# Adaptive layer norm, a state-space mixer and a top-2 mixture of experts: sixteen slots, a new beginning, statistics a step ahead, W2's sums and scaling moved

## The reference, cut to what matters

```python
mod = (silu(c) @ wmod).reshape(16, 6, 1, 128)        # sa, ca, ga, sb, cb, gb per sequence
h = layernorm(x) * (1 + ca) + sa
xi = silu(h @ Win + bin)                             # 256 channels
# h_t = 0.9 h_{t-1} + xi_t Bp;  y_t = h_t Cp + Dp xi_t   (a scan over 512 tokens)
x = x + ga * (y @ Wout + bout)
h = layernorm(x) * (1 + cb) + sb
p = softmax(h @ Wr + br); probs, idx = top_k(p, 2)   # 8 experts
for every expert e: r = layernorm(relu(h @ W1[e] + b1[e])) * g1[e] + be1[e]      # 512 wide
                    y_e = layernorm(relu(r @ W2[e] + b2[e])) * g2[e] + be2[e]    # 128 wide
x = x + gb * (sum over the two chosen experts of gate * y_e)
```

## Time and profile before

| what | value |
|---|---|
| median of 3 runs | 551.77 us (550.8 to 551.81) |
| the profiled execution, its own time | 549.6 us |
| its span, first to last instruction | 547.8 us |
| busy: TensorE, VectorE, ScalarE, GpSimd | 489.3, 472.3, 400.9, 384.5 us |
| mean granted TensorE clock | 0.969 of full |
| beginning, to the scan of batch 0 | 0 to 28.4 us |
| mixer, to the scan of batch 15 | 28.4 to 171.6 us |
| turn to the experts | 171.6 to 190.9 us |
| experts' tiles | 190.9 to 520 us |
| the end | 520 to 547.8 us |

### The profile page before, as it was taken

How to read it: one execution, slowest core, us unless ns; L and a number is a source line. 1 busy time by engine, 2 the same in 40 slices (tenths; PEclk the granted TensorE clock), 3 DMA queues, 4 the chain that set the end, 5 groups by cost and what they waited for, 6 DMA issues and landing times. The chain is left out here.

```text
span 547.8 us, 15172 instructions
## 1 busy us (share of the span) xinstructions
PE 489.3 (89%) x3075; PEld 389.0 (71%) x3075; DVE 472.3 (86%) x2217; ACT 400.9 (73%) x1107; POOL 384.5 (70%) x524
## 2 busy tenths in 40 slices
PE   2698897989896589899999999999999999999863
PEld 2264554555554469699999999999989899889740
DVE  5968899898988578598888899999999899999896
ACT  1435877587876357688888888888888798888763
POOL 4361477777777777866665668888888788769683
PEclk9999999999999589999999999999999999999996
DMA  6962011451111165454555555666666766666665
GB/s 176 309 186 77 31 54 50 95 111 54 55 50 54 55 174 134 136 151 138 143 146 145 173 144 177 179 187 161 182 186 151 181 193 159 184 182 195 189 180 154
DMA packets 79342, 77.81 MB, mean 142 GB/s; under 512 B 11086, under 2 KB 72681, under 8 KB 79126
## 3 DMA queue, kind: packets, MB, share of 16 engines
q1 hardware_dynamic: 70838, 59.92, 42.0%
q0 software_dynamic: 8416, 16.93, 8.7%
HBM read 54.65 MB, written 22.59 MB: 141 GB/s over the span
## 5 line engine op out<-in xcount | busy, mean ns | idle before, releaser
L577 POOL DMA_INDIRECT expert_results<-y,target x135 | 136.3, 1010 | 42.3 <-issue 41.0
L546 POOL DMA_INDIRECT expert_rows<-rows_ring,slot x128 | 123.4, 964 | 54.8 <-issue 53.6
L1344 PE MATMUL bank<-W,h2T 128*128 x1080 | 142.7, 275 | 0.7 <-ACT h2T L727 0.7
L1344 PEld LDWEIGHTS bank<-W,h2T 128*128 128x128 f32 x1080 | 131.2, 192 | 0.9 <-issue 0.9
L719 ACT ACTIVATE h1T<-bank 128x512 f32<-128x512 f32 x135 | 80.7, 598 | 44.6 <-PE bank L1329 43.6
L1108 DVE BATCH_NORM_STATS2 stf<-h1T 128x6 f32<-128x512 f32 x135 | 90.9, 673 | 0.0
L1335 PE MATMUL bank<-ident,h1T 128*128 128x128 f32 x540 | 80.9, 272 | 0.0
L1335 PEld LDWEIGHTS bank<-ident,h1T 128*128 128x128 f32 x540 | 67.3, 141 | 18.2
L727 ACT ACTIVATE h2T<-bank 128x512 f32<-128x512 f32 x135 | 79.6, 589 | 0.0
L1326 PE MATMUL bank<-b_parts,onesr 128*128 x135 | 65.3, 484 | 3.2 <-DVE h3lo L1100 3.2
L1084 DVE SCALAR_TENSOR_TENSOR wmod<-bank,rse,shifts 128x128 f32<-128x128 f32 x135 | 46.5, 344 | 20.5 <-PE bank L1344 7.1
(11 more groups left out here) (212 smaller groups left out, 1037.7 us busy)
## 6 DMA issues: line engine op xcount, KB each, us to landing
shifts<-expert_shifts SPq DMA_DIRECT2D x135, 192.0 KB
hrow<-expert_rows SPq DMA_DIRECT2D x135, 65.0 KB
xi<-expert_results SPq DMA_DIRECT2D x12, 512.0 KB, 5.1
X<-in_L_attn_x SPq DMA_DIRECT2D x8, 512.0 KB, 7.1
out_x<-X SPq DMA_DIRECT2D x15, 256.0 KB
expert_results<-y,target POOLq DMA_INDIRECT x135
shifts<-in_L_ffn_W SPq DMA_DIRECT2D x4, 512.0 KB, 6.4
expert_rows<-rows_ring,slot POOLq DMA_INDIRECT x128, 2.3
```

The source lines that it names most:

```text
L546: nc.gpsimd.indirect_dma_start(out=rows_d, out_offset=bass.IndirectOffsetOnAxis(ap=slot[q][:, n // TOPK, n % TOPK:n % TOPK + 1], axis=0), ...
L577: nc.gpsimd.indirect_dma_start(out=results_d, out_offset=bass.IndirectOffsetOnAxis(ap=target[n % TURN][:], axis=0), in_=y[k][:], in_offset ...
L1344: ins = mm(acc, rT[q][:, ch * P:(ch + 1) * P], W2[:, bass.ds(e2 * CF + ch, 1), :], start=(ch == 0), stop=(ch == CF - 1))
```

## The change

- **Sixteen slots.** Up to tile 31 shifts and y have 16 slots (`ring(i)`), the second eight in tiles that the mixer no longer needs (xi, mixT, scan, spare_gb). Semaphores of these loads and stores serve pairs of slots (`pair`, `pair_uses`). target has 32 buffers.
- **First round.** Four batches instead of three: 24 tiles. GROUP_ENDS is (4, 7, 10, 13, 14, 15, 16) instead of (3, 5, 8, 11, 14, 15, 16). GpSimd stores all rows of the last batch at once, with y additions of tiles 0 to 11 between the last two batches' stores, and stores two results per addition for tiles 12 to 17.
- **Pieces of the sum.** The 44 early pieces lie evenly over tiles 52 to 132 (`piece_tile`), loads and stores of X in SyncE's list follow them.
- **New beginning.** b1_parts is zeroed by ScalarE instead of GpSimd, b2_rows after VectorE's constants; c and wmod have semaphores of their own; X's first 256 KB come before the small loads and the next 256 KB behind them; batch 0's statistics and root come before the modulation (`first_norm`, `first_mods`); the modulation's products go to bank 4.
- **Statistics a step ahead.** The first statistics of batch s+3 stand between the dependent operations of step s's chain (`first_stats`, `first_mv`). n2 of batch s-1 is normalised in step s, half before h1T and half behind it, instead of in step s+1.
- **W2.** Sums one expert per step in steps 2 to 9, in bank 4, copied in two halves in steps 6 and 10 (`copy_sums`). Scaling in steps 12 to 18, five pieces a step between other operations (`scale_w2`).
- **half_gates.** The tanh and the table load of the gates stand behind the first h3hi instead of ahead of the experts.

The diff, cut to its core:

```diff
...
-    ROUND1_BATCHES = 3
-    GROUP_ENDS = (ROUND1_BATCHES, 5, 8, 11, 14, 15, 16)
+    ROUND1_BATCHES = 4
+    GROUP_ENDS = (ROUND1_BATCHES, 7, 10, 13, 14, 15, 16)
...
-        target = [sb(f"target_{n}", [P, 1], I32) for n in range(8)]
+        TARGETS = 32
+        target = [sb(f"target_{n}", [P, 1], I32) for n in range(TARGETS)]
...
+        FIRST_COMBINED, LAST_COMBINED = 52, EXPERT_TILES - 3
...
+        def piece_tile(b, j):
+            return FIRST_COMBINED + (b * J + j) * (LAST_COMBINED - FIRST_COMBINED) // (EARLY * J - 1)
+        def pieces_at(i):
+            return [(b, j) for b in range(EARLY) for j in range(J) if piece_tile(b, j) == i]
...
+        WIDE_UNTIL = 32
...
+        y += [xi_flat[0][:, n * D:(n + 1) * D] for n in range(RESULTS)]
+        mix_flat = mixT_both[:].rearrange("p q l -> p (q l)")
+        shift_rows = [shifts[:, n, :] for n in range(SLOTS)]
+        shift_rows += [of[:, n * 3 * D:(n + 1) * 3 * D] for of in (xi_flat[1], mix_flat) for n in range(2)]
+        shift_rows += [scan[0][:, 0:3 * D], scan[1][:, 0:3 * D], spare_gb[0][:, 0:3 * D], spare_gb[1][:, 0:3 * D].bitcast(F32)]
...
+        def ring(i):
+            return i % (2 * SLOTS) if i < WIDE_UNTIL else i % SLOTS
+        def pair(i):
+            return ring(i) // 2
...
+        def pair_uses(i):
+            return sum(pair(m) == pair(i) for m in range(min(i // 2 * 2 + 2, EXPERT_TILES)))
+        def last_user(i):
+            return max((m for m in range(i) if ring(m) == ring(i)), default=None)
...
+        SUMS_FROM, W2_FROM, W2_PIECES = 2, 12, 5
+        W2_STEPS = -(-E * CF // W2_PIECES)
...
-            sp.dma_start(X[:, 0:NX, :], x_v[:, 0:NX, :]).then_inc(x_loaded[0], 16)
+            sp.dma_start(X[:, 0:J, :], x_v[:, 0:J, :]).then_inc(first_x_loaded, 16)
...
+            sp.dma_start(X[:, J:NX, :], x_v[:, J:NX, :]).then_inc(x_loaded[0], 16)
...
             def load_shifts(i):
...
-                if i >= SLOTS:
-                    sp.wait_ge(y_ready, i + 1 - SLOTS)
-                sp.dma_start(shifts[:, i % SLOTS, :], shifts_d[bass.ds(e, 1), :].broadcast_to([P, 3 * D])).then_inc(shifts_loaded[i % SLOTS], 16)
...
+                if last_user(i) is not None:
+                    sp.wait_ge(y_ready, last_user(i) + 1)
+                sp.dma_start(shift_rows[ring(i)], shifts_d[bass.ds(e, 1), :].broadcast_to([P, 3 * D])).then_inc(shifts_loaded[pair(i)], 16)
...
-            for i in range(ROUND1, EARLY_TURN * SLOTS):
+            STORED_AT = {piece_tile(b, 0) + 23: b for b in range(EARLY - 2)}
+            LOADED_AT = {piece_tile(b, 0) + 1: b for b in range(EARLY)}
+            for i in range(ROUND1, EXPERT_TILES):
                 load_next(i)
-            for turn in range(EARLY_TURN, EARLY_TURN + EARLY):
-                for i in range(turn * SLOTS, min((turn + 1) * SLOTS, EXPERT_TILES)):
-                    load_next(i)
-                    if i % SLOTS == 1:
-                        load_early(turn - EARLY_TURN)
-                if turn - EARLY_TURN >= 2:
-                    store_early(turn - EARLY_TURN - 2)
+                if i in LOADED_AT:
+                    load_early(LOADED_AT[i])
+                if i in STORED_AT:
+                    store_early(STORED_AT[i])
...
-            nc.gpsimd.memset(b2_rows, 0.0).then_inc(pool_consts, 1)
-            nc.gpsimd.memset(b1_parts[:].bitcast(F32), 0.0).then_inc(pool_consts, 1)
-            pool.wait_ge(pool_consts, 7)
+            pool.wait_ge(dve_setup, SETUP_PADDING)
+            nc.gpsimd.memset(b2_rows, 0.0).then_inc(b2_zeroed, 1)
...
-            def add_shift(i, n, first):
-                k = n % RESULTS
...
                 pool.wait_ge(vs_ready, i + 1)
-                if not first:
-                    pool.wait_ge(results_stored[k], (i - k) * (16 // RESULTS))
-                nc.gpsimd.tensor_tensor(wide(y[k][:]), wide(vs[n % VS]), shifts[:, n:n + 1, 2 * D:3 * D], ALU.add).then_inc(y_ready, 1)
...
+                if last_user(i) is not None:
+                    pool.wait_ge(results_stored[k // 2], 16 * pair_uses(last_user(i)))
+                nc.gpsimd.tensor_tensor(wide(y[k]), wide(vs[i % VS]), wide(shift_rows[k][:, 2 * D:3 * D]), ALU.add).then_inc(y_ready, 1)
...
+            with pool.Fori(0, B // RING - 1) as four:
+                for k in range(RING):
+                    store_batch(four * RING + k, k)
+            for b in range(B - RING, B - 2):
+                store_batch(b, b % RING)
+            rows_of(B - 2)
+            for n in range(J * TOPK):
+                store_rows((B - 2) % RING, n)
+                if n % 2 == 1:
+                    add_shift(n // 2)
+            rows_of(B - 1)
+            for n in range(J * TOPK):
+                store_rows((B - 1) % RING, n)
+                add_shift(J + n)
...
+            ADDED = J + J * TOPK
+            for i in range(J):
+                store_results(i)
+            for i in range(ADDED, ADDED + ADDED // 2):
+                add_shift(i)
+                for n in range(2):
+                    store_results(J + 2 * (i - ADDED) + n)
+            BEHIND = ADDED + ADDED // 2
+            for i in range(BEHIND, LAST_SHIFTED):
+                for b, j in pieces_at(i):
+                    early_gb_of(b, j)
+                for b, j in pieces_at(i - 1):
+                    if b < EARLY - 1:
+                        early_out_of(b, j)
+                add_shift(i)
+                if i == BEHIND:
+                    store_results(i - 2)
+                store_results(i - 1)
...
+            act.wait_ge(dve_setup, SETUP_PADDING)
+            for e in range(E):
+                ins = nc.scalar.activation(b1_parts[:, e, :], padding[:, 0:1].broadcast_to([P, F]), ACT.Copy)
+            ins.then_inc(b1_zeroed, 1)
...
-                if on(s - 2, B):
-                    act.wait_ge(nm_ready, s + 2)
-                    normalise(s - 2, n2[q], 0, rs[1 - q], nm[1 - q], n2_ready)
...
+                if on(s - 1, B):
+                    act.wait_ge(nm_ready, s + 3)
+                    normalise(s - 1, n2[1 - q], 0, rs[q], nm[q], range(J // 2))
                 if on(s + 1, B):
...
+                if on(s - 1, B):
+                    normalise(s - 1, n2[1 - q], 0, rs[q], nm[q], range(J // 2, J)).then_inc(n2_ready, 1)
...
-            act.wait_ge(lead_ready, 1)
-            nc.scalar.activation(gate[:, 0, :], lead[:], ACT.Tanh, scale=0.5).then_inc(half_gate_ready, 1)
-            nc.scalar.activation(root_of_eps[:], eps[:], ACT.Sqrt)
+            def half_gates():
+                act.wait_ge(lead_ready, 1)
+                nc.scalar.activation(gate[:, 0, :], lead[:], ACT.Tanh, scale=0.5).then_inc(half_gate_ready, 1)
+                nc.scalar.activation(root_of_eps[:], eps[:], ACT.Sqrt)
...
+                if s == -1:
+                    half_gates()
...
+            def first_stats(b, j):
+                if j == 0:
+                    dve.wait_ge(x_loaded[b * XL // B] if b else first_x_loaded, 16)
+                ins = vec.bn_stats(st[b % 2][:, J + j, :], X[:, b * J + j:b * J + j + 1, :])
+                if j == J - 1:
+                    ins.then_inc(first_stats_ready, 1)
+            def first_mv(b):
+                dve.wait_ge(first_stats_ready, b + 1)
+                dve.nop(nofuse=True)
+                for j in range(J, 2 * J):
+                    ins = vec.bn_aggr(mv[b % 2][:, j, :], st[b % 2][:, j, :])
+                ins.then_inc(first_mv_ready, 1)
+            def scale_w2(s, m):
+                n = (s - W2_FROM) * W2_PIECES + m
+                if 0 <= n < E * CF:
+                    if n == 0:
+                        dve.wait_ge(sums_loaded, 16)
+                    ins = vec.scalar_tensor_tensor(W2[:, n:n + 1, :], W2[:, n:n + 1, :], g1T[:, n:n + 1],
+                                                   means[:, n // CF:n // CF + 1, :], ALU.mult, ALU.subtract)
+                    if m == W2_PIECES - 1 or n == E * CF - 1:
+                        ins.then_inc(w2_ready, 1)
+            def copy_sums(half):
+                part = slice(half * E // 2, (half + 1) * E // 2)
+                dve.wait_ge(sums_done, half + 1)
+                dve.wait_ge(b2_loaded, 16)
+                vec.tensor_tensor(w2_sums[:, part, :], bank[4][0:2, :].rearrange("k (e d) -> k e d", d=D),
+                                  b2_rows[:, part, :], ALU.add).then_inc(sums_copied, 1)
             def mixer_step(s, q, e, k):
...
-                if on(b, B):
-                    dve.wait_ge(x_loaded[b * XL // B], 16)
...
+                if s == SUMS_FROM + E // 2:
+                    copy_sums(0)
+                if s == SUMS_FROM + E:
+                    copy_sums(1)
...
+                if following:
+                    first_stats(s + 3, 0)
...
-                    vec.tensor_copy(rows[k3][:, :, D + 1], besti[p][:, :, 0]).then_inc(ids_ready, 1)
...
                     dve.wait_ge(mix_done, s)
```

(79 more changed lines are left out.)

202 lines of the change are left out of this document (77 added, 125 removed).

## The result

The changed kernel is slower: 555.66 us (median of 4 runs, 554.77 to 559.23) against 551.28 for the kernel before on the same chip, a ratio of 1.0125 with a 95% interval of 1.0081 to 1.017. The forecast was 540.3 with a range of 532.5 to 546.5, and slower had a chance of 0.05. The profiled execution has a span of 554.1 us, 6.3 more than before.

A forecast was written before the change was run, and what follows sets the result against it. The mixer was taken as bound by its 8.97 us step pace with no engine full, the experts by TensorE at 2.37 us a tile. Terms 7.3 + 0.4 + 1.4 - 0.5 + 3.8 - 0.9 = 11.5 gave 540.3 us, range 532.5 to 546.5.

The forecast's parts named there:

- beginning, to scan 2: Start of the mixer: earlier constants, X and nm of batch 0 move scan 2 from 51.42 to 44.1, 7.3 us won.
- pace, scan 2 to 15: Thirteen mixer steps: moved n2, statistics and W2 work give 116.2 against 116.6, the table's 3.6 staying; 0.4 us won.
- turn, to the first transpose: Mixer to experts: TensorE no longer waits for n2 (0.8) and the last W2 pair goes (0.6); 1.4 us won.
- first stall, tile 4 to 16: Early expert tiles: sixteen slots of shifts and a 24-tile first round remove both causes of the stall; 3.8 us won.
- tiles 16 to 134: Later expert tiles: SyncE's queue regains less between 512 KB loads, no fence holds; loss 5.4 becomes 6.3, -0.9 us.
- end: Behind the last expert tile: claimed untouched, no time won or lost.
- rival 2: Expert tiles: SyncE's queue falls behind and hrow comes late; 544.3 us with two loads more, 3.5 us gain with four; chance 0.17.
- Rival 4: Expert tiles: every one of eleven closer 512 KB loads holds hrow, 21 us more less 12.4; 560 us, chance 0.05.
- Rows on GpSimd: GpSimd's row stores, 162 us for 128, start 7.3 earlier and with twelve y additions end near 223.
- rival 5: Mixer to experts: the beginning's gain is waited for at GpSimd's rows, 8 us lost at tile 24; no change, chance 0.03.
- rival 1: Mixer: contention in steps 1 and 2 is hidden and fills of gaps are free; gain 18, 533.7 us, chance 0.22.
- rival 3: Mixer: gaps between chained VectorE operations hold nothing, each fill costs its whole 0.3, 3 to 4 us less; 543.9, chance 0.10.

The follow-up runs named there:

- own semaphores: The changed kernel, but loads of shifts have a semaphore for each slot modulo eight, so v0 waits for its own tile's load alone; 541.36 us, ratio 0.9876.
- the stores apart: Own semaphores for shifts, with stores of X 20 instead of 23 tiles behind their batch's first piece, so none directly follows a 512 KB load; 540.92 us, ratio 0.9859.
- the run with eight slots: Own semaphores for shifts, but shifts keep eight slots, a load waiting for y of the tile eight before; 545.13 us in one run.
- own semaphores for results: The changed kernel, but stores of results have a semaphore for each slot modulo eight, pairs kept for shifts; 555.58 us, ratio 1.0112.
- the run with n2 of batch 0 back: Own semaphores for shifts and the stores apart, with n2 of batch 0 normalised in its old place; 537.32 us, ratio 0.98.
- SHIFT_LAG = 3: The run with n2 of batch 0 back, but shifts loaded three tiles behind hrow instead of four; 535.81 us, ratio 0.9762.

## Why the prediction was wrong

Its sum against the two profiles; a plus is time won:

| step | forecast | seen | from |
|---|---|---|---|
| beginning, to scan 2 | 7.3 | 6.1 | 51.42 - 45.32 |
| pace, scan 2 to 15 | 0.4 | 1.3 | 120.22 - 118.93 |
| turn, to the first transpose | 1.4 | 1.2 | 19.30 - 18.10 |
| half_gates, to tile 4 | -0.5 | -0.45 | 10.14 - 10.59 |
| first stall, tile 4 to 16 | 3.8 | 3.2 | 32.40 - 29.18 |
| tiles 16 to 134 | -0.9 | -15.6 | 284.98 - 300.58 |
| end | 0 | -2.1 | 29.34 - 31.40 |
| sum | 11.5 | -6.3 | |

- **The step that failed** is the one on the experts. It took a slot's new semaphore at nothing: it asked whether the results land in time ("no fence holds") and what SyncE's list carries, and never what v0 waits for once two slots share a count. In its place the runs showed a wait for the second load of the pair, at 14 us when it is taken away and 14.5 when it is added to the kernel before. Its price could be bounded before: in the kernel before v0 of a tile starts 3.3 us or more after its load's issue, and the next tile's load is issued 2.2 later. If a load takes 3.2 us to be of use, then wherever the lead is under 5.4 us an even tile can be late, and from tile 16 on 95 of 119 leads are. With own semaphores the span is 539.5, 8.3 us less than before where the sum had 11.5, and most of the missing 3.2 are SyncE's late stalls (2.8); the beginning lacks 1.3 and the pace has 0.9 more than forecast.
- **SyncE's late stalls** were mis-sized beside it: 0.9 forecast, 3.7 seen with own semaphores. The forecast counted loads and stores, but not that six of the new places coincide (tiles 75, 82, 97, 112, 119 and 127). The prediction had the right wait, hrow behind 512 KB. With the stores apart the two traces lose 5.0 and 4.8, less than the 5.4 before. This is rival 2's mechanism, late hrow, and its size is near what was seen: 4 us less for two late loads more.
- **Rival 4** named the right sign for the wrong reason. By it each 512 KB load holds hrow; in the changed kernel TensorE waits for hrow once, 0.7 us, and v0 for shifts 15.4 us. With own semaphores hrow is late behind five of the eleven loads, 4.95 us in all, not behind all of them.
- **The beginning.** nm of batch 0 stood at 8.49 (forecast 8.7) and scan 0 at 20.56 (21). Scan 2 came 1.2 us later than forecast: the forecast had neither the wait for X nor h1T behind n2 of batch 0. The first alone gave nothing when it was taken away, and nm of step 1 stood at 32.60 in spite of it (forecast 32.5); the second gave 0.9 to 2.0. The chained operation of 0.65 was read too widely: in the trace before, those beside GpSimd's W1lo take 0.65 and those beside its W1hi 0.30.
- **Rows on GpSimd** end at 229.2 and not near 223, later than the 222.9 of the kernel before, with additions between them. Tile 24, the first of the second round, starts at 241.3 without a wait, so rival 5 was out.
- **The pace** was near in its sum (0.4 forecast, 1.3 seen) by luck, for its parts were wrong. From scan to scan the last steps take 8.7 to 9.1 us and those with a sum 8.7 to 9.6, so the steps won nothing. The gain is the first round's table: the two steps that have it take 11.86 and 7.62, together 1.5 more than two steps of 9, where the forecast kept the 3.6 us. The thirteen steps fit neither rival 1 (3 us less for free gaps) nor rival 3 (3 to 4 us more); the price of a statistic in a gap stays unknown.
- **First stall.** 3.2 seen, and 3.8 with own semaphores, as forecast; of the two reasons that the forecast gave, sixteen slots of shifts were not needed, as the run with eight slots shows.
- **The end** was forecast at nothing and lost 2.1. With own semaphores for shifts it takes 29.2 us again, with own semaphores for results and the pairs kept 29.5, so the pair wait is not shown as its cause, and the cause stays open.

## What to carry to other kernels

Who shares a semaphore between two transfers makes the first consumer wait for the second transfer. Price it as one issue interval taken off the lead of every first consumer, and look up the smallest lead in the trace. Where the semaphores don't go round, share between transfers that are far apart (eight tiles here), with the issuer waiting for the earlier one, and don't share between neighbours. When transfers are moved to a new rhythm, list where two big ones meet, and look at every consumer behind them: here the rows of a tile came late, not only the shifts that had been suspected.

## What was not expected of the hardware

In step 1 of the run with n2 of batch 0 back, VectorE's ve, a sum with a constant over 128x8, took 2.79 us and began and ended with GpSimd's W1lo, which is four subtractions of 0.72 us in a row (the row of VectorE, then that of GpSimd):

```profile
28.72 2.79 DVE L1068 TENSOR_SCALAR ve<-mv 128x8 f32<-128x8 f32 x1
```

```profile
28.72 2.76 POOL L576 TENSOR_TENSOR W1lo<-shifts,W1hi 128x256 fp32r<-128x256 f32 x4
```

The same instruction took 0.66 in the changed kernel and 0.72 in the same kernel with SHIFT_LAG = 3, whose beginning is the same: about one subtraction. So what a chain pays under the split differs between executions of the same work, by 2 us for one operation here. The Trainium skill, SBUF — State Buffer, "Who interferes with whom", lists operations with a constant among those that can contend with GpSimd for a shared pair of ports, and says that whoever issues first shuts the other out for the whole instruction. The 0.66 and 0.72 agree with that, one instruction of 0.72 each; that VectorE stood through four of them is more than the page says.
